# Twice x less its mean: from a TensorE product to VectorE, in the stage that joins the two halves of a graph layer

## What is computed

```python
flow = jnp.concatenate([past_agg, future_agg], axis=1)          # N x 128
out = leaky_relu(flow @ Wc1 + bc1) @ Wc2 + bc2                    # N x 64
L0 = out + x
x1 = layernorm(x + L0)        # (v - mean(v)) / sqrt(var(v) + eps) over 64 features, v = out + 2x
```

## Time and profile before

| what | value |
|---|---|
| median of 3 runs | 7769.36 us |
| the profiled execution, its own time | 7782.76 us |
| its span in the trace | 7780.6 us |
| TensorE matmuls, busy | 6823.7 us (88%) |
| VectorE, busy | 4508.9 us (58%) |
| ScalarE, busy | 2236.1 us (29%) |
| GpSimd, busy | 5902.6 us (76%) |
| granted TensorE clock, mean | 0.773 of full |
| the joining stage in the trace | 5170.8 us (first instruction) to 5440.2 us (last) |

### The profile page before, as it was taken

The page is one execution under the profiler, slowest core; times in us unless marked ns, Lnnn a source line. Parts: engine busy times, 40 slices in busy tenths (PEclk is TensorE's granted clock), DMA queues, the critical chain, the costliest instruction groups (busy, mean ns, idle before and its releaser), DMA issues. The chain is left out here.

```text
span 7780.6 us, 143006 instructions
## 1 busy us (share of the span) xinstructions
PE 6823.7 (88%) x40496; PEld 5317.8 (68%) x40496; DVE 4508.9 (58%) x17274; ACT 2236.1 (29%) x4908; POOL 5902.6 (76%) x4690
## 2 busy tenths in 40 slices
PE   5889888989889999889889889989799996999993
PEld 4777777878777787778778778766455554555552
DVE  5777777777777777633333333333666664666663
ACT  2222222222222222222222222224443334333333
POOL 5888888888888888888888888852678884888873
PEclk7777777776777777766776676666999996999995
DMA  4333333333333333222222222222333334333342
GB/s 131 34 34 34 34 34 33 34 34 34 34 34 34 34 34 34 32 27 28 27 27 27 27 28 27 27 54 77 84 77 75 73 74 71 74 73 76 74 70 54
DMA packets 716773, 374.06 MB, mean 48 GB/s; under 512 B 550948, under 2 KB 666948, under 8 KB 716210
## 3 DMA queue, kind: packets, MB, share of 16 engines
q0 software_dynamic: 319648, 158.18, 20.4%
q1 hardware_dynamic: 394399, 210.89, 10.7%
q10 hardware_dynamic: 2482, 2.00, 0.1%
HBM read 289.60 MB, written 81.09 MB: 48 GB/s over the span
## 5 line engine op out<-in xcount | busy, mean ns | idle before, releaser
L666 POOL DMA_INDIRECT future<-sbuf,sidx x1564 | 2492.8, 1594 | 484.2 <-issue 459.7
L652 POOL DMA_INDIRECT gbuf<-in_x_dram,gidx x1564 | 1607.4, 1028 | 482.9 <-issue 472.1
L1545 PE MATMUL bank<-at_dst,rows 128*128 128x512 bf16 x3136 | 1203.1, 384 | 0.5 <-ACT rows L1512 0.5
L1547 PE MATMUL bank<-at_dst,rows 128*128 128x512 bf16 x3136 | 1200.4, 383 | 0.0
L1512 ACT CAST rows<-bank 128x384 bf16<-128x384 f32 x1568 | 751.1, 479 | 1227.7 <-PE bank L1531 1226.4
L1396 POOL DMA_INDIRECT gb<-x,nidx x640 | 787.2, 1230 | 263.1 <-issue 140.5
L1396 POOL DMA_INDIRECT gb<-h,nidx x640 | 791.0, 1236 | 244.1 <-issue 142.6
L1434 DVE TENSOR_SCALAR at_dst<-iota,metaf 128x512 bf16<-128x512 f16 x3136 | 939.8, 351 | 2.4 <-PE bank L1547 1.2
L978 PEld LDWEIGHTS bank<-w1pe,featT 96*128 96x128 f32 x3128 | 724.3, 269 | 306.7 <-issue 306.1
L979 PE MATMUL bank<-w1px,srcT 65*128 65x128 f32 x3128 | 817.5, 355 | 0.0
L978 PE MATMUL bank<-w1pe,featT 96*128 96x128 f32 x3128 | 817.4, 355 | 0.0
(11 more groups left out here) (260 smaller groups left out, 11247.1 us busy)
## 6 DMA issues: line engine op xcount, KB each, us to landing
laneb<-lanes SPq DMA_DIRECT2D x448, 224.0 KB
gbuf<-in_x_dram,gidx POOLq DMA_INDIRECT x1564
comb<-in_edge_attr_dram SPq DMA_DIRECT2D x391, 64.0 KB
future<-sbuf,sidx POOLq DMA_INDIRECT x1564, 3.2
blkb<-blkrow SPq DMA_DIRECT2D x240, 98.0 KB
future<-zero POOLq DMA_DIRECT2D x16, 800.0 KB, 17.7
fut<-future SPq DMA_DIRECT2D x100, 125.0 KB
gb<-x,nidx POOLq DMA_INDIRECT x644, 3.1
```

The costliest lines, as they stand in the source:

```text
L652: pool.indirect_dma_start(out=gbuf[:, b, q, :], out_offset=None, in_=x[:, :], in_offset=bass.IndirectOffsetOnAxis(ap=gidx[:, b, q:q + 1], ...
L666: pool.indirect_dma_start(out=future[q][:, :], out_offset=bass.IndirectOffsetOnAxis(ap=sidx[:, b, q:q + 1], axis=0), in_=sbuf[:, b, q, :], ...
L1545: pe.matmul(psHM[i % 2][:, :], rows16[:, j % AR, t % 2, 0:2 * D], at_dst[:, t % DR, :], start=(b == 0), stop=(b == BLOCKS - 1))
L1547: pe.matmul(psL[i % 2][:, :], rows16[:, j % AR, t % 2, 2 * D:4 * D], at_dst[:, t % DR, :], start=(b == 0), stop=(b == BLOCKS - 1)).then_in ...
```

## The change

The product with x goes. SyncE loads the chunk of x as it lies in the input (`x_c`, 125 rows of 1024 bytes), into `xn`. VectorE sums each node's 64 features (`xsum`), scales the sum by 2/64, and forms `xm` = 2x less that; these three instructions stand behind `leaky` of the same chunk. GpSimd adds the centred bias, now a tile `bcrow` of 125 equal rows, to `xm` (`add_bias`). VectorE empties `psO` with an addition of `xm` into `yc`, and ScalarE squares `yc` instead of reading PSUM twice. TensorE's `centred` is left with the four products of the hidden layer. TensorE's wait for `psO` to be empty is now a wait for VectorE.

```diff
--- before.py
+++ after.py
@@ -161,3 +161,3 @@
         wc2c = sb("wc2c", [H, D])
-        xc = sb("xc", [D + 1, D])
+        bcrow = sb("bcrow", [CP, D])
         wlr = sb("wlr", [D, 2, 2 * D])
@@ -393,3 +393,3 @@
                 pe.matmul(bank[7][:, 0:D], wc2T[:, :], centre[:, :], start=True, stop=True)
-                pe.matmul(bank[7][0:1, D:2 * D], bc2col[:, :], centre[:, :], start=True, stop=True).then_inc(s_wc, 1)
+                pe.matmul(bank[7][0:CP, D:2 * D], bc2col[:, :].to_broadcast([D, CP]), centre[:, :], start=True, stop=True).then_inc(s_wc, 1)
 
@@ -422,3 +422,2 @@
                 dve.wait_ge(s_centre, 1)
-                dve.tensor_scalar(xc[0:D, :], centre[:, :], 2.0, None, ALU.mult)
 
@@ -484,3 +483,3 @@
                 dve.tensor_copy(wc2c[:, :], bank[7][:, 0:D])
-                dve.tensor_copy(xc[D:D + 1, :], bank[7][0:1, D:2 * D])
+                dve.tensor_copy(bcrow[:, :], bank[7][0:CP, D:2 * D])
                 dve.wait_ge(sA_t, CHUNKS)
@@ -1003,2 +1002,3 @@
         out_c = out.rearrange("(c p q) d -> c p (q d)", p=CP, q=CQ)
+        x_c = x.rearrange("(c p q) d -> c p (q d)", p=CP, q=CQ)
         future_c = [f[0:N, :].rearrange("(c p q) d -> c p (q d)", p=CP, q=CQ) for f in future]
@@ -1025,4 +1025,5 @@
         fut = tmp("fut", [CP, NB, TILES, CQ * D])
-        fsum, past, flow, hidc, xT_b, yc, sq, var, rows, spread_b = buffers(
-            "c", ("fsum", CP, CQ * D), ("past", D, CH), ("flow", 2 * D, CH), ("hidc", H, CH), ("xTb", D + 1, CH),
+        fsum, past, flow, hidc, xn, xm, xsum, yc, sq, var, rows, spread_b = buffers(
+            "c", ("fsum", CP, CQ * D), ("past", D, CH), ("flow", 2 * D, CH), ("hidc", H, CH), ("xn", CP, CQ * D),
+            ("xm", CP, CQ * D), ("xsum", CP, CQ),
             ("yc", CP, CQ * D), ("sq", CP, CQ * D), ("var", CP, CQ), ("rows", CP, CQ * D), ("spread", D, CH))
@@ -1034,6 +1035,7 @@
         (c_turned, c_lane, c_lane_st) = [tsem(f"c_lane{i}") for i in range(3)]
-        (c_ones, c_s1, c_s2, c_sum, c_P, c_C, c_past, c_max, c_inv, c_I, c_flow, c_F, c_fT, c_H, c_hb, c_hc, c_O, c_yc,
-         c_sq, c_var, c_sd, c_rs, c_rows, c_T, c_x1T, c_spread) = [tsem(f"c_{i}") for i in range(26)]
+        (c_s1, c_s2, c_sum, c_P, c_C, c_past, c_max, c_inv, c_I, c_flow, c_F, c_fT, c_H, c_hb, c_hc, c_O, c_yc,
+         c_sq, c_var, c_sd, c_rs, c_rows, c_T, c_x1T, c_spread) = [tsem(f"c_{i}") for i in range(25)]
         c_fut = [tsem(f"c_fut{b}") for b in range(NB)]
-        c_xT = [tsem(f"c_xT{b}") for b in range(NB)]
+        (c_xsum, c_xmean, c_xm, c_xb) = [tsem(f"c_x{i}") for i in range(4)]
+        c_xn = [tsem(f"c_xn{b}") for b in range(NB)]
         c_st = [tsem(f"c_st{b}") for b in range(NB)]
@@ -1053,4 +1055,4 @@
                     if c >= NB:
-                        sp.wait_ge(c_O, c - NB + 1)
-                    sp.dma_start(xT_b[0:D, c % NB, :], xT[:, c * CH:(c + 1) * CH]).then_inc(c_xT[c % NB], 16)
+                        sp.wait_ge(c_xm, c - NB + 1)
+                    sp.dma_start(xn[:, c % NB, :], x_c[c]).then_inc(c_xn[c % NB], 16)
 
@@ -1085,4 +1087,9 @@
 
+                def add_bias(c):
+                    v = by_slot(xm[:, c % NB, :])
+                    pool.wait_ge(c_xm, c + 1)
+                    pool.tensor_tensor(v, v, bcrow[:, :].unsqueeze(1).to_broadcast([CP, CQ, D]), ALU.add).then_inc(c_xb, 1)
+
                 pool.memset(acc[0:D, N:NA], 0.0)
-                stages(None, sum_tables, None, clear_sums)
+                stages(None, sum_tables, None, clear_sums, add_bias)
 
@@ -1090,3 +1097,2 @@
             def _(dve):
-                dve.memset(xT_b[D:D + 1, :, :], 1.0).then_inc(c_ones, 1)
                 dve.tensor_single_scalar(ranked[:, :, :], rank16[:, :, :], float(P), ALU.is_le).then_inc(c_left, 1)
@@ -1136,2 +1142,23 @@
 
+                def centre_x(c):
+                    b = c % NB
+                    if c >= NB:
+                        dve.wait_ge(c_yc, c - NB + 1)
+                    dve.wait_ge(c_xn[b], 16 * (c // NB + 1))
+                    dve.tensor_reduce(xsum[:, b, :], by_slot(xn[:, b, :]), AX_X, ALU.add).then_inc(c_xsum, 1)
+                    dve.wait_ge(c_xsum, c + 1)
+                    dve.tensor_scalar(xsum[:, b, :], xsum[:, b, :], 2.0 / D, None, ALU.mult).then_inc(c_xmean, 1)
+                    dve.wait_ge(c_xmean, c + 1)
+                    dve.scalar_tensor_tensor(out=by_slot(xm[:, b, :]), in0=by_slot(xn[:, b, :]), scalar=2.0,
+                                             in1=per_node(xsum[:, b, :]), op0=ALU.mult, op1=ALU.subtract).then_inc(c_xm, 1)
+
+                def centred(c):
+                    b = c % NB
+                    if c >= NB:
+                        dve.wait_ge(c_rows, c - NB + 1)
+                        dve.wait_ge(c_sq, c - NB + 1)
+                    dve.wait_ge(c_xb, c + 1)
+                    dve.wait_ge(c_O, c + 1)
+                    dve.tensor_tensor(yc[:, b, :], psO[0:CP, 0:CQ * D], xm[:, b, :], ALU.add).then_inc(c_yc, 1)
+
                 def leaky(c):
@@ -1142,2 +1169,6 @@
 
+                def both(c):
+                    leaky(c)
+                    centre_x(c)
+
                 def variance(c):
@@ -1160,3 +1191,3 @@
 
-                stages(None, past_side, past_mean, leaky, None, variance, normal)
+                stages(None, past_side, past_mean, both, centred, variance, normal)
                 leftover()
@@ -1188,7 +1219,5 @@
                     if c >= NB:
-                        act.wait_ge(c_rows, c - NB + 1)
                         act.wait_ge(c_var, c - NB + 1)
-                    act.wait_ge(c_O, c + 1)
-                    act.activation(sq[:, b, :], psO[0:CP, 0:CQ * D], ACT.Square).then_inc(c_sq, 1)
-                    act.copy(yc[:, b, :], psO[0:CP, 0:CQ * D]).then_inc(c_yc, 1)
+                    act.wait_ge(c_yc, c + 1)
+                    act.activation(sq[:, b, :], yc[:, b, :], ACT.Square).then_inc(c_sq, 1)
 
@@ -1225,3 +1254,2 @@
                 last.then_inc(c_turned, 1)
-                pe.wait_ge(c_ones, 1)
                 pe.wait_ge(c_lane, 4)
@@ -1265,3 +1293,2 @@
                     b = c % NB
-                    pe.wait_ge(c_xT[b], 16 * (c // NB + 1))
                     pe.wait_ge(c_hc, c + 1)
@@ -1271,4 +1298,3 @@
                         o = psO[0:CP, q * D:(q + 1) * D]
-                        pe.matmul(o, natural(hidc[:, b, :])[:, q, :], wc2c[:, :], start=True, stop=False)
-                        last = pe.matmul(o, natural(xT_b[:, b, :])[:, q, :], xc[:, :], start=False, stop=True)
+                        last = pe.matmul(o, natural(hidc[:, b, :])[:, q, :], wc2c[:, :], start=True, stop=True)
                     last.then_inc(c_O, 1)
```

## The result

Before and after were run in turns on one chip. The median went from 7771.3 us (4 runs, 7762.4 to 7774.3) to 7697.7 us (4 runs, 7689.6 to 7709.2). The ratio is 0.9904, with a 95% interval of 0.9890 to 0.9918, so the changed kernel is faster by 64 to 85 us, about 1%. The forecast was 7700. The profiled execution took 7695.1 us, its span is 7693.3.

The account below looks back on a forecast made before the run. Joining-stage turn: longest of TensorE 7.0, transfers 7.2 and loop 6.3 us, taken as 7.3. Savings 64.7 + 5.4 - 0.4 = 69.7 us from 7782.8 give 7713; the median lies 13.4 lower, so 7700, range 7681 to 7731.

Parts of the forecast that it names:

- The removed products: Joining stage, TensorE: four of eight short products go, 0.45 us each, 1.80 us a turn, from 10.24 to 8.44 us.
- The clock: TensorE in the joining stage: less pecking keeps the clock up for 0.7 of the work that feels it, turn 7.0 us.
- The transfers: Joining stage DMA: six 125-row transfers, 6.45 us, and one of 64 rows, 0.75 us, set a floor of 7.2 us a turn.
- The sum: Joining stage: turn 7.3 us, saving 64.7 us over 22 turns, 5.4 in the last blocks, -0.4 at the end; together 69.7.
- VectorE, ScalarE and GpSimd: New work on x in the joining stage: VectorE's turn 5.3 us, GpSimd's addition 0.86 us, costing nothing while turns exceed 6.3 us.
- The loop: VectorE's 5.3 us plus ScalarE's squaring and emptying of the hidden layer, 1.06 us: 6.3 us a turn, below the transfers' 7.2.
- The clock that stays: Rival 1, chance 0.22: TensorE's clock pattern in the joining stage is unchanged; turn 8.44 us, saving 44.6 us, time 7725.
- rival 3: Joining stage: VectorE and GpSimd get in each other's way; loop 7.7 us, saving 60 us, time 7709; chance 0.10.
- No change: Rival 4, chance 0.05: joining stage transfers go at 84 GB/s, 9.9 us a turn, saving 12 us, time 7757.
- slower by the transfers: Rival 5, chance 0.04: joining stage 125-row transfers run at 57 GB/s, turn 14.2 us, 83 us lost, time 7852.
- rival 2: Joining stage: transfers are no floor and the clock stays up; turn 6.3 to 6.9 us, time 7684; chance 0.10.
- What the profile was to show: Joining stage: clock above 0.8, DMA share well above 0.29; prediction wrong if a turn is below 6.9 or above 7.8 us.

Follow-up runs that it names:

- six products: Changed kernel with two of its four short products a turn issued twice: 7711.0 us, ratio 0.9934, turn 6.97 us but for two of 8.2 and 8.6.
- no load of x: Changed kernel loading x for the first three chunks only, so five 125-row transfers a turn in place of six: 7690.6 us, ratio 0.9911, turn 6.83 us.
- seven 125-row transfers a turn: Changed kernel storing each chunk of finished rows a second time, into a table written over later: 7714.8 us, ratio 0.9925, turn 7.96 us after the first seven.
- the fastest version: Changed kernel with counts moved before past side on TensorE and each load of futures cut into 112 and 13 rows: 7703.6 us, ratio 0.9891, stage 183.2 us.

## Why the prediction was right, point by point

- **The removed products: right.** 0.45 us each, forecast and measured (5278.45 to 5280.23 for four, at the upper level). For the lower level the only rows are those of the kernel before, with the same pace. They give 25 x 1.80 = 45 of the 81 us.
- **The clock: right in kind and near in size.** A turn of 7.0 us was forecast between 6.14 and 8.44, and it is 6.83. The all-upper turn is 6.06. The clock gives the other 22 x 1.61 = 35 us. The reason that I gave, that a shorter stretch of short products leaves the clock less cause to fall, does not stand: with six products the clock fell in two turns of 19, with four in every second turn, with eight in each.
- **The transfers: the term that was mis-sized.** "7.2 us" for six 125-row transfers and one of 64 rows was too high. The changed kernel turned over in 6.83 without being held by them (no load of x: same turn), and where they do hold the turn it is 6.89. The 64-row store was counted with 0.75 us of its own; it runs for the most part on engines that the others leave idle, as the windows show: 156 GB/s at a share of 0.53 while it is under way, 117 at 0.34 without. The Trainium skill ("DMA: Bandwidth & Descriptors", "Why a DMA increments its semaphore by 16 and not by 1") had this right: a transfer takes the largest number of engines that divides its rows. By that rule 112 rows take all 16 engines and 13 rows 13, and the trace agrees as far as the share goes, from 39.4% to 47.3%. The 6.5 that the prediction put beside the 7.2 is 0.4 too low: six times 128 KB at 119 GB/s are 6.45 us. Give the store 5/16 of its 128 KB on the same five engines, and the sum at 119 GB/s is 6.8 us with six transfers and 7.9 with seven, an estimate by the same rule, beside 6.89 and 7.96 measured.
- **The sum.** The turn was set at 7.3 from the 7.2 and an allowance for near bounds; measured 6.83. So the stage was to lose 69.7 us and lost 81.1: 22 x 0.47 = 10.3 of the difference lie in the turn. Had the transfers stood at 6.9, the sum would have gone by TensorE's 7.0: so 0.30 of the 0.47 are the transfers and the allowance, and 0.17 are the clock, whose share was taken as 0.7 where 6.83 comes to 0.76. The median came out at 7698 against 7700 nevertheless, because the rest of the program moves by that much from one execution to the next. The agreement to 2 us is luck; the agreement to 11 us is the mechanism.
- **VectorE, ScalarE and GpSimd: right.** The addition from PSUM took 421 ns (forecast 430), the sum of x 409 (410), its scaling 261 (180), 2x less the mean 478 (430), GpSimd's addition 727 (860). The loop was put at 6.3 us; it shows at 6.47 once all else is out of the way. That agreement is partly luck: the forecast had the rows at 0.43 us, and in that run they take 0.94. Cost of it all in the changed kernel: at most 3.3 us.
- **The rivals.** The clock that stays (8.44 us a turn) is refuted by the timeline. Contention did not decide here: leaky's mean is 831 ns where it was 856, beside more work of GpSimd, and TensorE waits for it for only 1.8 us in the whole stage. The mechanism of rival 3 is there all the same, in the kernel before too (leaky above 0.68 only with an addition of GpSimd under way at its start), and it takes the 0.51 us a turn in the fastest version. No change and slower by the transfers are out: the rate rose to 130 GB/s. Nearest to what happened in the stage was rival 2, with a turn of 6.3 to 6.9 us, which I gave 0.10; but its reason, transfers that are no floor, holds only in that TensorE's 6.83 came out level with it.
- **What the profile was to show.** Clock above 0.8: 0.87. DMA share well above 0.29: 0.40. A turn below 6.9 was to count against the forecast, and it was 6.83, so by that test the working failed where the time did not.

**Left open** is why the clock falls with eight and with four short products and hardly ever with six (2 turns of 19), or with four when counts and past side change places (1 of 19). The turn's length changed in each of these along with the order, and no run held one of them fixed.

## What to carry to other kernels

When an engine that is busy all the time loses work, read the clock ahead of the count of products: here 1.80 us of products gave 3.41 us a turn. Then look for the bounds just below the new pace, since several may lie within half a us: lifting one of them gave nothing twice, and lifting both gave 9 us. The next bound then was an instruction that took twice its time beside another engine, so compare an instruction's longest with its median before its time goes into a sum. Count transfers by the engines that their rows can use, and let ones of another shape run beside them.

## What the runs showed that I had not expected

More work on TensorE can cost less than it takes: 0.14 us in 17 turns of 19 for two products of 0.45, and half their price over the stage, while the mean clock rose from 0.87 to 0.96. And a queue can be full at a DMA share of 0.39: with seven 125-row transfers a turn TensorE waited for data while the 16 engines were on average less than half in use; cutting 125 rows into 112 and 13 raised the share, with both edits to 0.49.
